# A state space scan kernel: two channel tiles at a time instead of four, six PSUM banks in the ring instead of four

## What is computed

```
for i in range(N_LAYERS):                        # 2
    xz = rmsnorm(x) @ in_w ; xb, z = split(xz)    # 512 channels each
    xb = silu(causal_conv(xb))
    delta, B, C = split(xb @ xp_w)                # B, C: 16 states
    delta = softplus(delta @ dtw + dtb)
    v_t = 0.6 * v_(t-1) + delta * B_t * xb        # per channel and state
    h_t = exp(delta * -exp(a_log)) * h_(t-1) + v_t
    y_t = sum over the 16 states of h_t * C_t
    x = x + ((y + dp * xb) * silu(z)) @ out_w
```

## Time and profile before

| | us |
|---|---|
| median of 3 runs | 1668.32 (1667.53 to 1669.48) |
| the profiled execution | 1670.65 |
| its span in the trace | 1669.2 |
| the eight items, in the trace | 74.83 to about 1096 |
| one item, 1 to 6 each | 129.7 to 129.8 |

### The profile page before, as it was taken

The page is one execution under the profiler, slowest core; times in us unless marked ns, Lnnn a source line. Parts: engine busy times, 40 slices in busy tenths (PEclk is TensorE's granted clock), DMA queues, the critical chain, the costliest instruction groups (busy, mean ns, idle before and its releaser), DMA issues.

```text
span 1669.2 us, 44666 instructions
## 1 busy us (share of the span) xinstructions
PE 1436.8 (86%) x19348; PEld 1002.1 (60%) x19348; DVE 1112.7 (67%) x1540; ACT 899.5 (54%) x1287; POOL 919.3 (55%) x769
## 2 busy tenths in 40 slices
PE   5778788889889979979979888888889888899997
PEld 2456566666666657657656666653343433479997
DVE  4288698588588688678768767977667673242223
ACT  3756557557457566566555654622646467334440
POOL 1268578777777786886976968861030300015541
PEclk8899999999999999999999999997999999999999
DMA  4000010001101000100100112445060500602224
GB/s 165 5 27 28 27 47 33 27 27 53 53 27 52 29 27 28 53 27 27 53 27 27 59 59 78 83 85 127 1 114 1 102 1 1 254 29 69 70 67 170
DMA packets 36882, 93.57 MB, mean 56 GB/s; under 512 B 8273, under 2 KB 21073, under 8 KB 32337
## 3 DMA queue, kind: packets, MB, share of 16 engines
q1 hardware_dynamic: 30128, 74.72, 14.8%
q0 software_dynamic: 6048, 14.95, 3.5%
q10 hardware_dynamic: 512, 1.05, 0.4%
HBM read 64.35 MB, written 9.57 MB: 44 GB/s over the span
## 4 chain that ended last, share of the span: by engine, by line
PE 53%; DVE 31%; issue 9%; ACT 4%; DMA 2%; POOL 1%; DVEq 0%; SPq 0%; ACTq 0%
PE psum L571 12%; DVE hst L730 8%; DVE hst L734 5%; DVE hst L736 5%; PE psum L472 4%; PE psum L549 4%; PE psum L1644 4%; PE psum L1656 3%; PE psum L1232 3%; PE psum L514 2%; PE psum L503 2%; PE psum L1214 2%; DVE w_early L730 2%; PE psum L540 2%; PE psum L1586 2%
## 5 line engine op out<-in xcount | busy, mean ns | idle before, releaser
L928 POOL TENSOR_TENSOR hst<-hst,cb 128x512 f32<-128x512 f32 x399 | 511.5, 1297 | 213.7 <-DVE hst L730 154.6
L730 DVE TENSOR_TENSOR_SCAN hst<-dA,psum 128x512 f32<-128x512 f32 x249 | 294.7, 1207 | 145.2 <-PE psum L571 144.6
L549 PE MATMUL psum<-ident,hst 128*128 128x128 f32 x1596 | 240.4, 281 | 0.0
L871 ACT ACTIVATE dA<-delta,alog 128x512 f32<-128x512 f32 x256 | 177.1, 717 | 66.8 <-DVE hst L736 24.8
L549 PEld LDWEIGHTS psum<-ident,hst 128*128 128x128 f32 x1596 | 176.4, 141 | 59.3 <-issue 37.6
L871 ACT ACTIVATE dA<-xres,alog 128x512 f32<-128x512 f32 x256 | 176.4, 717 | 48.5 <-DVE hst L736 20.9
L571 PE MATMUL psum<-filt,c_early 64*64 64x86 f32 (+1 forms) x6144 | 144.5, 239 | 65.6 <-DVE hst L736 28.8
L1353 DVE TENSOR_REDUCE nmax<-psum 128x2 f32<-128x1024 f32 x128 | 154.6, 1219 | 57.7 <-PE psum L1198 57.3
L571 PE MATMUL psum<-filt,uT 64*64 64x86 f32 (+1 forms) x6144 | 142.6, 237 | 52.0 <-DVE hst L736 23.6
L571 PEld LDWEIGHTS psum<-filt,c_early 64*64 64x64 f32 x6144 | 125.2, 134 | 102.7 <-issue 44.4
L1282 ACT ACTIVATE pT<-psum 128x1024 f32<-128x1024 f32 x128 | 127.9, 1024 | 102.3 <-PE psum L1218 79.1
(11 more groups left out here) (244 smaller groups left out, 2357.8 us busy)
## 6 DMA issues: line engine op xcount, KB each, us to landing
cb<-c_rows SPq DMA_DIRECT2D x32, 1024.0 KB, 4.7
qk_first<-w_early SPq DMA_DIRECT2D x64, 64.0 KB, 2.4
qk<-part SPq DMA_DIRECT2D x64, 64.0 KB, 2.6
w_up<-up_dram SPq DMA_DIRECT2D x8, 512.0 KB, 7.4
w_down<-down_dram SPq DMA_DIRECT2D x8, 512.0 KB, 13.4
w_up<-y_choice SPq DMA_DIRECT2D x8, 512.0 KB, 7.2
qk<-part POOLq DMA_DIRECT2D x48, 64.0 KB, 5.3
qk_first<-part SPq DMA_DIRECT2D x40, 64.0 KB, 2.4
```

Source lines behind the costliest of these rows:

```text
L549: m = pe.matmul(psum[:, Y0 + et, t * P:(t + 1) * P], hst(i)[:, t * P:(t + 1) * P], ident[:], start=n == 0 and t == 0, stop=n == NSTATE - 1 ...
L730: dve.tensor_tensor_scan(hst(i), a, v, 0.0, ALU.mult, ALU.add).then_inc(scan_done, 1)
L871: act.activation(dA[:, a % NDA, :], delta[k % 2][:, et, :], ACT.Exp, scale=alog[:, k // B, et, n:n + 1]).then_inc(decay_done, 1)
L928: pool.tensor_tensor(h, h, cb[:, q % 2, state_of(i)[1] % GN, :], ALU.mult).then_inc(g_done, 1)
```

## The change

1. The order of the state tiles: an item goes through its 16 states for channel tiles 0 and 1 (steps 0 to 31), then again for 2 and 3 (steps 32 to 63).
2. So only two sums are open at a time. They take two banks, and the ring gets six (`NRING`, `Y0`).
3. A bank of the sums is used again in mid-item: PE's first addition of tiles 2 and 3 waits for the copy `y` of tiles 0 and 1. `plan_mid` places their `y` (ACT, steps 37 and 39), `bt` (PE 39, 41), `xd` (DVE 40, 42) and `gate` (POOL 40, 42). Those of tiles 2 and 3 stay at the start of the next item.
4. The filters must last the whole item: nine slots of two states each in place of two of four; POOL makes 64 small ones in place of 32 large ones, those of the next item from step 34 on.
5. C is loaded twice per item, a load for every eight tiles in place of sixteen: 64 loads of 1 MB in place of 32. SP's queue is written anew for that.

```diff
-            filt = sb(mc, "filt", [P, 2, NCH, GN, QC])
+            filt = sb(mc, "filt", [P, NFILT, NCH, 2, QC])
             yT = xraw
             cb = sb(mc, "cb", [P, 2, GN, S])
             c_rows = nc.dram_tensor("c_rows", [NI, NSTATE, S], F32).ap()
-            NDA, AHEAD, LAG, NRING, Y0 = 5, 4, 7, 4, 4
+            NDA, AHEAD, LAG, NRING, Y0 = 5, 4, 7, 6, 6
             NH = LAG + 2
 
...
             def state_of(i):
                 k, r = i // TILES, i % TILES
-                return k, r // (2 * ET) * 2 + r % 2, r // 2 % ET
+                turn, r = r // (EP * NSTATE), r % (EP * NSTATE)
+                return k, r // (2 * EP) * 2 + r % 2, turn * EP + r // 2 % EP
+
+            def use_of(i):
+                return i // (GN * EP)
+
+            def filter_after(f):
+                k, pair = f // NPAIRS, f % NPAIRS
+                return TILES * k + EP * NSTATE + (pair + 1) * 2 * EP
 
             dA = sb(mc, "dA", [P, NDA, S])
             hst_own = sb(mc, "hst", [P, NH - 2, S])
...
@@ -361,13 +371,21 @@
                     put("dve", "xd", e)
                     if at != "last" or e % 2 == 0:
                         put("pool", "gate", e)
-                    s -= e < ET - 1
+                    s -= at == "last" and e < ET - 1
                 for t in range(TB):
                     s = s + 1 if at == "last" else ((17, 19, 21, 23) if at == NI - 1 else (11, 13, 15, 16))[t]
                     put("pe", "bo", t)
                     s += 1
                     put("dve", "add", t)
                     s -= at == "last"
+
+            def plan_mid(k):
+                for e in range(EP):
+                    s = EP * NSTATE + LAG - 2 * EP + 2 + 2 * e
+                    steps["act"].setdefault((k, s), []).append((k, "y", e))
+                    steps["pe"].setdefault((k, s + 2), []).append((k, "bt", e))
+                    steps["dve"].setdefault((k, s + 3), []).append((k, "xd", e))
+                    steps["pool"].setdefault((k, s + 3), []).append((k, "gate", e))
 
             def plan_norms(at, s, g):
                 def put(engine, *name):
...
                 if k:
-                    plan_back(k - 1, k, LAG - ET)
+                    plan_back(k - 1, k, LAG - 2)
                 else:
                     s = plan_norms(k, 1, 0)
                     plan_norms(k, TILES - 16, 1)
+                plan_mid(k)
                 if k + 1 < NI:
                     plan_front(k + 1, k, s)
                 else:
...
             def pe_add_state(i):
                 k, n, et = state_of(i)
                 pe.wait_ge(g_done, i + 1)
-                if k and n == 0:
-                    pe.wait_ge(y_out, ET * (k - 1) + et + 1)
+                if n == 0 and ET * k + et >= EP:
+                    pe.wait_ge(y_out, ET * k + et + 1 - EP)
                 for t in range(TB):
-                    m = pe.matmul(psum[:, Y0 + et, t * P:(t + 1) * P], hst(i)[:, t * P:(t + 1) * P], ident[:],
+                    m = pe.matmul(psum[:, Y0 + et % EP, t * P:(t + 1) * P], hst(i)[:, t * P:(t + 1) * P], ident[:],
                                   start=n == 0 and t == 0, stop=n == NSTATE - 1, is_transpose=True, skip_group_check=True)
                 if n == NSTATE - 1:
                     m.then_inc(y_full, 1)
...
-                    n2 = n // 2 * 2 % GN
-                    f = NG * k + n // GN
+                    f = NPAIRS * k + n // 2
                     if i % TILES == 0:
                         pe.wait_ge(bank_act, emptied_by("act", k, "c" if k else "ch", NCH - 2))
-                    if i % (GN * ET) == 0:
+                    if i % (2 * EP) == 0:
                         pe.wait_ge(filt_done, f + 1)
                     if i % 2 == 0:
...
                 pe_side(k, "bt", ET - 1)
                 bks = [pe_open(k, "bo", t) for t in range(TB)]
                 pe.wait_ge(ld_wout, 32)
                 for kt in range(ET):
-                    if kt % 2:
-                        pe.wait_ge(gated_dve, kt // 2 + 1)
+                    if kt == ET - 1:
+                        pe.wait_ge(gated_dve, 1)
                     else:
-                        pe.wait_ge(gated, ET * k + kt // 2 + 1)
+                        pe.wait_ge(gated, ET * k + kt + 1)
                     for t in range(TB):
                         m = pe.matmul(bks[t][:, 0:D], sz[k % 2][:, kt, t * P:(t + 1) * P], w_out[k // B][:, kt, :], start=kt == 0, stop=kt == ET - 1)
                         if kt == ET - 1:
...
+                    act.copy(yT[:, j, :], psum[:, Y0 + j % EP, :]).then_inc(y_out, 1)
                 elif what == "dbc":
                     act.wait_ge(bank_full, filled(k, "xp", 0))
...
                     pool.tensor_tensor(sz[par][:, j, :], sz[par][:, j, :], xbs[par][:, j, NSTATE:NSTATE + S], ALU.mult).then_inc(gated, 1)
 
             def pool_filter(f):
-                k, g = f // NG, f % NG
+                k, pair = f // NPAIRS, f % NPAIRS
                 if f == 0:
                     pool.wait_ge(ld_scan, 64)
-                pool.wait_ge(bank_dve, emptied_by("dve", k, "dbcT", 0))
-                if f >= 2:
-                    pool.wait_ge(v_full, VINC // 2 * GN * ET * (f - 1))
-                pool.tensor_tensor(filt[:, f % 2], toep[:, :].unsqueeze(1).unsqueeze(1).to_broadcast([P, NCH, GN, QC]),
-                                   bcol[:, k % 2, :, g * GN:(g + 1) * GN].unsqueeze(3).to_broadcast([P, NCH, GN, QC]),
+                if pair == 0:
+                    pool.wait_ge(bank_dve, emptied_by("dve", k, "dbcT", 0))
+                if f >= NFILT:
+                    pool.wait_ge(v_full, VINC // 2 * filter_after(f - NFILT))
+                pool.tensor_tensor(filt[:, f % NFILT], toep[:, :].unsqueeze(1).unsqueeze(1).to_broadcast([P, NCH, 2, QC]),
+                                   bcol[:, k % 2, :, 2 * pair:2 * pair + 2].unsqueeze(3).to_broadcast([P, NCH, 2, QC]),
                                    ALU.mult).then_inc(filt_done, 1)
+
+            FEARLY = 3
 
             def pool_mamba():
                 pool.memset(uw, 0.0).then_inc(zeroed, 1)
...
-                pool_filter(0)
+                for f in range(FEARLY):
+                    pool_filter(f)
                 for i in range(NI * TILES):
-                    q = i // (GN * ET)
-                    if i % (GN * ET) == 0:
-                        if q + 1 < NI * NG:
-                            pool_filter(q + 1)
+                    k, r = i // TILES, i % TILES
+                    q = use_of(i)
+                    if i < EP * NSTATE and r % (2 * EP) == 0 and FEARLY + r // (2 * EP) < NPAIRS:
+                        pool_filter(FEARLY + r // (2 * EP))
+                    if k + 1 < NI and r >= EP * NSTATE and r % (2 * EP) == 2:
+                        pool_filter(NPAIRS * (k + 1) + (r - EP * NSTATE) // (2 * EP))
+                    if i % (GN * EP) == 0:
                         pool.wait_ge(ld_c[q % 2], 16 * (q // 2 + 1))
...
             def sp_c_load(q):
-                k, g = q // NG, q % NG
-                if g == 0:
+                k, g = q // NUSE, q % NG
+                if q % NUSE == 0:
                     sp.wait_ge(c_stored, 16 * (k + 1))
                 if q >= 2:
-                    sp.wait_ge(g_done, GN * ET * (q - 1))
+                    sp.wait_ge(g_done, GN * EP * (q - 1))
                 sp.dma_start(cb[:, q % 2], c_rows[k, g * GN:(g + 1) * GN, :].partition_broadcast(P)).then_inc(ld_c[q % 2], 16)
 
...
+                    sp_c_load(NUSE * k + 2)
+                    sp_c_load(NUSE * k + 3)
                     if k == NI - 1:
                         sp.wait_ge(decay_done, TILES * (NI - 1))
                         sp.wait_ge(bank_full, filled(NI - 2, "bo", TB - 1))
                         for b in range(B):
                             sp.dma_start(xres[:, toks(b), :], x_tok[:, toks(b), :]).then_inc(ld_xres[b], 16)
-                    sp_c_load(NG * k + 2)
+                    if k + 1 < NI:
+                        sp_c_store(k + 1)
+                    sp_c_load(NUSE * k + 4)
                     if k == NI - 1:
                         sp.wait_ge(gated, ET * (NI - 1))
                         sp.wait_ge(bank_dve, emptied_by("dve", k, "ak", 1))
                         for dst, src in first_strips(1):
                             sp.dma_start(dst, src).then_inc(early_k, 16)
-                    sp_c_load(NG * k + 3)
-                    if k == NI - 1:
-                        sp.wait_ge(bank_dve, emptied_by("dve", k, "aq", 1))
-                        for dst, src in first_strips(0):
-                            sp.dma_start(dst, src).then_inc(early_q, 16)
+                    sp_c_load(NUSE * k + 5)
                     if k == B - 2:
                         sp.wait_ge(bank_full, filled(B - 1, "z", ET - 1))
                         sp.dma_start(w_in, d["w_in"][:, 1]).then_inc(ld_win[1], 16)
@@ -993,10 +1020,15 @@
                         for name in ("w_q", "w_k"):
```

(11 more changed lines are left out.)

16 lines of the change are left out of this document (9 added, 7 removed).

## The result

| | before | changed |
|---|---|---|
| median, us | 1667.92 (1667.32 to 1669.48, 4 runs) | 1578.62 (1573.89 to 1580.34, 4 runs) |
| profiled execution, us | 1670.65 | 1579.04 |
| its span, us | 1669.2 | 1577.5 |
| ratio of the times | | 0.9459, 95% interval 0.9437 to 0.948 |

The change takes 89 us off, where 56 were forecast. One of the four executions of split2, further down, took 2730.6 us, far from its other three; that kernel's figures go by those three.

A forecast was written before the change was run, and what follows sets the result against it. No engine bounds a whole item; PE and DVE hand the time over through a ring of four. Six items -56, item 0 -6, last item +7, end -1: -56 on the median 1668.32 gives 1612 us, range 1583 to 1648.

The forecast's parts named there:

- The mechanism: Ring between PE and DVE: with four banks PE waits for the scans, with six it has one pair more in hand.
- the third that was named: Sign of being right: the rows of PE waiting for scans before `v` fall to a third.
- first and last stretch of an item: Item 4, 598.52 to 615.32 and 707.11 to 728.24: from 37.93 to 30.2 us, a gain of 7.7.
- 28.5 if POOL's tail is swallowed elsewhere: Lower end for the first and last stretch together, where 30.2 us was taken and 33.5 was the upper end.
- PE is the floor: Rival, 12%: items 1 to 6 come to PE's 113.58 and some 2 us, -14 each, total 1580 us.
- 615 to 656, and 681 to 707: Item 4's stretches with PE 94% busy: gains 1.1 (0 to 2.4) and 0.7 (-1 to 1.5) us.
- The stretch with the new wait: Item 4, 656.13 to 681.20, 25.07 us: ACT's mid-item copy waits for DVE's last `max`; no gain, +0.2 us.
- The prediction's case that all four `max` might take 1.71: Softplus stretch, POOL fuller by two filters: 1.8 us more an item, and 1612 would become 1625.
- Item 0: First item, 134.47 us: a gain between 3.8 and 9.3 us, taken as 6.
- The last item: POOL waits some 12.7 us for C behind the strips; +12.6 after, -5.6 on the way there, net +7 (+4 to +11).
- The end: Output projection after the last item: half can start at once with six banks, -1 us.
- The slower case: Rival, 8%: the mid-item wait at steps 37 to 40 runs all six banks empty; at 9.5 us an item, 1679 us.

The follow-up runs named there:

- split2: The changed kernel with every fourth pair scanned in halves too, 190 tiles in place of 100: 1583.09 us, ratio 0.9473.
- own_lag5: own_y with PE adding a state tile five tiles behind instead of seven: 1592.32 us, ratio 0.953, 117.4 us an item.
- filt2: The changed kernel with each small filter made twice into the same place, about 9 us more of POOL an item: 1630.99 us, ratio 0.9767.
- ring4: The changed kernel with four banks in the ring, two left idle: 1711.92 us, ratio 1.027, 134.3 us an item.
- own_y: The changed kernel with the mid-item copies `y` of items 0 to 6 in memory that needn't wait for the last `max`: 1585.79 us, 116.8 an item.
- late_filt: The changed kernel with the next item's filters made at steps 46 to 60 instead of 34 to 62: 1575.22 us, ratio 0.9431.
- best: The changed kernel with the edits of own_y and late_filt, and the last item's C load for tiles 40 to 47 before the strips: 1558.95 us.

## Why the prediction was wrong, and where it was right

**The mechanism was right.** The ring's depth carries the gain: 17.0 us an item by the fifth bank, 1.7 by the sixth, none by the order with four. These 18.7 are more than the 14.1 by which the change beats the kernel before, since the changed kernel with four banks is 4.5 us an item slower than that one, by its wait at mid-item. Pairs with one `c` piece between them start every 2.94 us (655.41, 658.35), against 3.70 before; 3.0 to 3.1 had been named. Of the waits for scans even less is left than the third that was named. PE in the changed kernel's item 4:

```profile
655.41 1.12 PE L589 MATMUL psum<-filt,c_early 64*64 64x86 f32 x48
...
658.35 1.12 PE L589 MATMUL psum<-filt,c_early 64*64 64x86 f32 x48
```

**The step that failed: first and last stretch of an item.** The prediction took POOL's floor of 29.9, put both stretches at 30.2 from 37.93, and gained 7.7; they came to 26.9 and gained 11.0. The durations in that sum were good (the small filter was taken at 1.1 and takes 1.06). What failed is the charge: all products of the tiles whose `v` pairs lie in these stretches were put on them. POOL's timeline isn't cut there. What bounds these stretches now is PE, busy 9.68 + 16.74 = 26.4 of 26.9 us, as in the rival "PE is the floor", whose total came true; POOL does not. In the stretch before them it is busy 25.65 of 25.73 (21.15 of 25.91 before), and in the two themselves 9.96 + 14.18 = 24.1 of 26.9. The prediction had named this itself as the lower end ("28.5 if POOL's tail is swallowed elsewhere") and then took a value near the upper floor. own_lag5 and filt2 show what binds POOL in its place, two dates. The end itself was too high as well: it stood above a PE floor of about 28, worked out from PE's busy times before, and the same stretches now take 26.4. Three of the four `bt` have left the first stretch and not two (16 matmuls of 2.51 us before, 4 of 0.60 now; the third stands behind the cut at 555.34), which is 1.9 of the 2.5 us by which PE's busy time fell.

**615 to 656, and 681 to 707.** Forecast 1.1 and 0.7, measured 2.1 and 0.2. Inside the ends given.

**The stretch with the new wait.** Forecast +0.2, measured -1.15. The chain came as described: the last `max`, ACT's copy behind it, PE's addition behind that, the `v` pair for the third `z`.

```profile
615.62 0.59 ACT L805 COPY xraw<-psum 128x512 f32<-128x512 f32 x1 [3.93 <-DVE delta L666]
```

```profile
616.35 0.63 PE L568 MATMUL psum<-ident,hst 128*128 128x128 f32 x4 [1.30 <-ACT xraw L805]
...
617.94 1.12 PE L589 MATMUL psum<-filt,c_early 64*64 64x86 f32 x48 [0.53 <-ACT sz L792]
```

Its size was 1.2 too large. The copy began 21.6 us after the stretch's start, where 22.4 had been worked out, and the pair 23.9, where 25.1 had. By the trace most of the difference is DVE: the `max` products took 0.88 us on average from 330 to 900 us, 1.14 before. DVE at these steps:

```profile
610.26 0.66 DVE L666 TENSOR_TENSOR delta<-delta,xraw 128x512 f32<-128x512 f32 x1
...
611.97 0.66 DVE L666 TENSOR_TENSOR delta<-delta,xraw 128x512 f32<-128x512 f32 x1
...
614.03 1.51 DVE L666 TENSOR_TENSOR delta<-delta,xraw 128x512 f32<-128x512 f32 x1
```

POOL at the same time:

```profile
612.01 1.75 POOL L953 TENSOR_TENSOR hst<-hst,cb 128x512 f32<-128x512 f32 x1
613.72 1.26 POOL L910 TENSOR_TENSOR overlay<-delta,xbs 128x512 f32<-128x512 f32 x1
614.95 1.71 POOL L953 TENSOR_TENSOR hst<-hst,cb 128x512 f32<-128x512 f32 x1
```

The prediction's case that all four `max` might take 1.71 didn't come true: one of these four took 1.51, and the others 0.66 to 0.78, though POOL was busy 96% of the stretch. By the Trainium skill (SBUF — State Buffer, two separate sides), of a DVE operation with two SBUF inputs and a GpSimd operation the one that starts first has the shared ports for its whole length, and the other is blocked. The trace agrees with that rule. The `max` at 611.97 starts 0.04 before POOL's product; it takes 0.66, and the product 1.75 where 1.26 is usual. The `max` at 614.03 starts 0.31 behind a product and takes 1.51, 0.56 beyond that product's end. So the later one pays, and only what is left of the first. The prediction's case had charged every `max` with nearly a whole product.

**Item 0.** Forecast -6, measured -12.0. The value between 3.8 and 9.3 came from the failed step; item 0 gained as much as the others, less 2.1.

**The last item.** Forecast +7 (4 to 11), measured +3.3. The wait for `cb` was 13.97 where 12.7 had been worked out, the way to the strips -7.5 where -5.6 had; what followed the strips grew by 10.8 in place of 12.6.

**The end.** Forecast -1, measured -1.4: the output projection starts at 1004.85, right behind the last `bt` and with no wait, where it had stood 1.15 us.

**Not foreseen:** +2.8 us in attention and experts. PE is busy 505.25 us there, where it had 501.94. The mean granted clock is 0.95 in both. Each kernel's own executions lie 2 to 6 us apart, so that nothing can be told from it.

In sum the items failed, -14.1 each against -9.3, which is 29 of the 36 us between -92 and -56, and item 0 with the same cause another 6. The slower case, in which the wait at mid-item drains the ring, needed 8 us an item; ring4 shows that the mechanism is there (4.7 us an item with four banks). With six it doesn't drain the ring; taking it away gains nothing by itself (own_y), and 1.4 us an item once the filters are moved too (late_filt 115.2, best 113.8).

## What to carry to other kernels

If the chain passes between a producer and a consumer through a ring, vary the ring's depth first: here the fifth bank took 17 us of 134, the sixth 2, and with four banks the reordering was worth nothing. The sum of an engine's work over a stretch is no bound for that stretch if the engine may trail; look for the dates it has to keep, and what stands before each. Where two waits end within a microsecond or two of each other, taking one away shows nothing, and both must be taken away together before either is called worthless.
